# First attention of a gated cross-attention kernel: setup in 64-row bands, turned value-output rows, loads in halves, mask written by ScalarE

## The reference, cut to what matters

```
q = layernorm(x) @ wq[h] + bq[h];  k = ctx @ wk[h] + bk[h];  v = ctx @ wv[h] + bv[h]
scores = where(mask[b, s, t], q @ k.T / sqrt(64), -1e9)
out    = concat_h(softmax(scores) @ v) @ wo + bo
x      = x + tanh(g_xattn[0]) * out
```

## Time and profile before

| | |
|---|---|
| median of 3 runs | 776.97 us (775.05 to 778.43) |
| the profiled execution | 778.79 us, its span 777.0 us |
| TensorE busy | 735.8 us, 95% of the span |
| DVE, ACT, POOL busy | 415.7, 255.4, 120.4 us |
| mean granted TensorE clock | 0.983 |
| first weight-fed matmul | 5.93 us |
| first scores matmul of the first attention | 45.88 us |
| one tile in the steady loop | 10.80 us |

### The profile page before, as it was taken

The page is one execution under the profiler, slowest core; times in us unless marked ns, Lnnn a source line. Parts: engine busy times, 40 slices in busy tenths (PEclk is TensorE's granted clock), DMA queues, the critical chain, the costliest instruction groups (busy, mean ns, idle before and its releaser), DMA issues. The chain is left out here.

```text
span 777.0 us, 11690 instructions
## 1 busy us (share of the span) xinstructions
PE 735.8 (95%) x3507; PEld 500.0 (64%) x3508; DVE 415.7 (53%) x1020; ACT 255.4 (33%) x544; POOL 120.4 (16%) x129
## 2 busy tenths in 40 slices
PE   6989999999989999799999999999999999999991
PEld 6857776677754344589998756555665665665661
DVE  5868766776734475998889443212333333333330
ACT  1532323222245444657776331111211211221220
POOL 4100000000000000100000005540223223223222
PEclk9999999999999999999999899999999999999997
DMA  9534000000014000029001102322222322322221
GB/s 305 139 124 152 0 0 1 0 0 0 0 60 158 0 0 1 1 96 339 0 0 55 28 1 96 111 82 69 41 48 41 48 48 41 47 48 41 45 37 20
DMA packets 42401, 45.11 MB, mean 58 GB/s; under 512 B 8404, under 2 KB 36134, under 8 KB 42372
## 3 DMA queue, kind: packets, MB, share of 16 engines
q1 hardware_dynamic: 35028, 34.99, 14.4%
q0 software_dynamic: 7344, 9.75, 7.6%
HBM read 27.91 MB, written 16.79 MB: 58 GB/s over the span
## 5 line engine op out<-in xcount | busy, mean ns | idle before, releaser
L408 PE MATMUL ps<-middle,work 128*128 128x256 f32 (+3 forms) x824 | 217.7, 410 | 2.2 <-ACT work L960 1.5
L960 ACT ACTIVATE work<-ps 128x256 f32<-128x256 f32 (+5 forms) x263 | 100.9, 420 | 343.7 <-PE ps L411 315.9
L408 PEld LDWEIGHTS ps<-middle,work 128*128 128x128 f32 x824 | 152.1, 190 | 42.4 <-issue 23.6
L408 PE MATMUL ps<-early,work 128*128 x312 | 141.1, 595 | 0.8 <-ACT work L960 0.8
L411 PE MATMUL ps<-consts_sb,work 128*128 128x128 f32 (+1 forms) x672 | 99.1, 282 | 13.0 <-ACT work L960 3.9
L411 PEld LDWEIGHTS ps<-consts_sb,work 128*128 128x128 f32 (+1 forms) x672 | 78.6, 142 | 48.6 <-issue 28.3
L408 PEld LDWEIGHTS ps<-early,work 128*128 128x128 f32 x312 | 57.8, 190 | 61.7 <-issue 60.5
L408 PE MATMUL ps<-late,work 32*128 32x154 f32 (+3 forms) x704 | 81.8, 309 | 2.3 <-DVE x_rows L1471 1.1
L1702 DVE COPY work<-ps 128x256 f32<-128x256 f32 x39 | 16.6, 425 | 117.7 <-PE ps L411 117.7
L408 PE MATMUL ps<-early,late 128*128 128x512 f32 (+2 forms) x192 | 78.1, 611 | 0.3 <-ACT early L1061 0.3
L372 POOL TENSOR_TENSOR rstd<-var_eps,minus_half 128x8 f32<-128x8 f32 (+2 forms) x8 | 13.4, 1672 | 415.6 <-DVE var_eps L1270 415.6
(11 more groups left out here) (159 smaller groups left out, 608.8 us busy)
## 6 DMA issues: line engine op xcount, KB each, us to landing
early<-in_w SPq DMA_DIRECT2D x16, 512.0 KB, 10.3
expert_rows<-work SPq DMA_DIRECT2D x39, 130.0 KB, 2.7
work<-expert_rows SPq DMA_DIRECT2D x39, 130.0 KB, 2.1
middle<-in_w SPq DMA_DIRECT2D x8, 512.0 KB, 8.1
x_rows<-in_x SPq DMA_DIRECT2D x4, 512.0 KB, 9.4
out_rows<-x_rows SPq DMA_DIRECT2D x4, 512.0 KB, 3.1
late<-in_ws SPq DMA_DIRECT2D x3, 512.0 KB, 3.8
early<-in_wv SPq DMA_DIRECT2D x1, 1024.0 KB, 9.4
```

Source lines behind the costliest of these rows:

```text
L408: return nc.tensor.matmul(o, l, r, start=start, stop=stop, **kw)
L960: return nc.scalar.activation(o, i, ACT.Copy)
```

## The change

In the setup, `kbd` and `zv` go. K and V are written whole to `ks` and `vs` (one DVE addition a bank in place of four), and each head is multiplied alone: a `unit(n)` does its three or two pairs as two bands of 64 rows, one head each, both batches side by side (154 columns), the two bands into two banks. ACT evicts the even heads (`even_rows`), DVE the odd ones (`odd_rows`). Units 0 to 5 make `gk`; units 6 to 11 make the value side transposed, `voT`, and 40 transposes on TensorE (`turn_out`, ten groups of two chunks) turn it into `vo`, evicted seven groups by ACT and three by DVE. Units 8 to 11 and the turns come after the first tile's scores.

The row bq . k goes too, with its splitting and its DMAs. Instead each row of `wq_s` is shifted so that it sums to bq (`shift`, from row sums by ACT with an accumulator and by DVE), and ACT adds 1.0 to each transposed normed tile. Since a normed row sums to zero, the shift alone adds nothing, and the 1.0 adds bq . k.

The mask is converted by POOL, turned once by 16 bf16 matmuls of 77 columns into `seed0`, and ACT copies a tile's 77 columns (`pick`) and writes them, spread over the heads, into the scores' banks before the f32 matmuls add to them (`seeds0`). Only the first tile keeps the bf16 mask matmul. Loads of K, V and Q come in halves, x in four parts, and the statistics of x are made in three parts (two tiles a batch in the setup, the others after the first and the second tile's step). Four matmuls on zeros (`warm`) open TensorE's program.

```diff
 # SyncE
-            for a, z in ((0, 3 * P), (3 * P, H * DK)):
-                sp.dma_start(wk_s[:, :, a:z], wk0[:, a:z].rearrange("(k p) n -> p k n", p=P)).then_inc(q[f"ld_k{a // 384}"], 16)
-            sp.dma_start(wv_s, wv0.rearrange("(k p) n -> p k n", p=P)).then_inc(q["ld_v"], 16)
-            sp.dma_start(wq_s, wq0T.rearrange("(j p) n -> p j n", p=P)).then_inc(q["ld_q"], 16)
+            weights(wk_s, wk0, 0, "ld_k0")
+            weights(wk_s, wk0, 1, "ld_k1")
+            sp.dma_start(wq_s[:, 0:4, :], wq_rows[:, 0:4, :]).then_inc(q["ld_q"], 16)
+            weights(wv_s, wv0, 0, "ld_v0")
+            tiles(0, 2, "ld_x0")
+            weights(wv_s, wv0, 1, "ld_v1")
+            sp.dma_start(wq_s[:, 4:8, :], wq_rows[:, 4:8, :]).then_inc(q["ld_q2"], 16)
             sp.dma_start(wo_s, wo0.rearrange("(j p) n -> p j n", p=P)).then_inc(q["ld_o"], 16)
...
 # GpSimd
-            nc.gpsimd.memset(zv.rearrange("p b n -> p (b n)"), 0.0).then_inc(q["pool_fill"], 1)
-            nc.gpsimd.memset(mlhs[:], 1.0).then_inc(q["pool_fill"], 1)
+            nc.gpsimd.tensor_copy(id_bf, ident[0:NK, 0:NK]).then_inc(q["mask_done"], 1)
+            pool.wait_ge(q["ld_mask"], 32)
+            nc.gpsimd.tensor_scalar(mlhs[:], mask_u8[:], BIG, -BIG, ALU.mult, ALU.add).then_inc(q["mask_done"], 1)
+            pool.wait_ge(q["su_shift"], 2)
+            for j in (6, 7):
+                nc.gpsimd.tensor_tensor(wq_s[:, j, :], wq_s[:, j, :], shift[:, j:j + 1].to_broadcast([P, D]),
+                                        ALU.add).then_inc(q["su_w2"], 1)
...
 # TensorE
+            def unit(n):
+                after(pe, q["su_ea"], FREE_EVEN[n])
+                after(pe, q["su_ed"], FREE_ODD[n])
+                u, m = n % 6 // 2, n % 2
+                left, right = ((wq_s, ks), (wo_s, vs))[n // 6]
+                j0, j1 = 3 * u, min(3 * u + 3, PAIRS)
+                for j in range(j0, j1):
+                    for r in range(2):
+                        rows = slice(64 * r, 64 * r + 64)
+                        last = mm(ps[:, UNIT_BANKS[n][r], PW * (j - j0):PW * (j - j0) + PW],
+                                  left[rows, j, P * m:P * m + P], right[rows, j, :])
...
                 for u, (a, z) in enumerate(UNITS):
-                    after(pe, q["n_sub"], 3 * t - 2 + u)
                     n = NK * (z - a)
+                    if seeded:
+                        pe.wait_ge(q["n_seed"], 3 * t - 2 + u)
+                    else:
+                        mm(ps[:, u, 0:n], mlhs[:, p, 0:P], spread(id_bf, 1, [NK, z - a, NK]), True, True)
                     for m in range(KD):
-                        mm(ps[:, u, 0:n], xnT[p][:, m, :], gk[:, p, m, NK * a:NK * z], m == 0, False)
-                    mm(ps[:, u, 0:n], mlhs[:, p, bass.ds((i + k // 2) * P, P)], mrhs[p][:, NK * a:NK * z],
-                       False, True).then_inc(q["n_sc"], 1)
+                        last = mm(ps[:, u, 0:n], xnT[p][:, m, :], gk[:, p, m, NK * a:NK * z], False, m == KD - 1,
+                                  skip_group_check=True)
+                    last.then_inc(q["n_sc"], 1)
...
             xt0(0, 0)
-            step0(0, 0, prev=False)
+            scores0(0, 0, seeded=False)
+            xt0(0, 1)
+            for n in range(8, 12):
+                unit(n)
+            for g in range(len(TURNS)):
+                turn_out(g)
+            scores0(0, 1)
...
 # ScalarE, in each step of the loop
+            def seeds0(i, k, units):
+                t = 2 * i + k
+                if units[0] == 0:
+                    act.wait_ge(q["n_seeds"], 3)
+                    copy(pick[:, k % 2, :], seed0[:, bass.ds(tile_of(i, k), 1), :].rearrange("p a n -> p (a n)")
+                         ).then_inc(q["n_pick"], 1)
+                    act.wait_ge(q["n_pick"], t)
+                for u in units:
+                    a, z = UNITS[u]
+                    act.wait_ge(q["n_sub"], 3 * t - 2 + u)
+                    copy(ps[:, u, 0:NK * (z - a)].rearrange("p (h t) -> p h t", t=NK),
+                         spread(pick[:, k % 2, :], 1, [P, z - a, NK])).then_inc(q["n_seed"], 1)
...
                 if nxt:
                     ev_xt(i, k + 1)
+                    seeds0(i, k + 1, (0, 1))
                 exps(i, k, "n", DK ** -0.5)
+                if nxt:
+                    seeds0(i, k + 1, (2,))
```

More of the change, by code:

```diff
@@ L426, in _ @@
[L426 to L434 removed]
+            project(0, 0)
+            pe.wait_ge(q["ld_k1"], 16)
+            project(0, 1)
@@ new lines, in _ @@
+            act.wait_ge(q["ld_q"], 16)
+            for j in range(4):
+                last = nc.scalar.activation(cut(middle, D * j, [D]), wq_s[:, j, :], ACT.Copy, accum_out=wsum[:, j:j + 1])
+            last.then_inc(q["su_wsum"], 1)
+            act.wait_ge(q["su_shift"], 1)
+            shifted(0, 4)
+            for n in range(3):
+                act.wait_ge(q["n_seed_mm"], n + 1)
+                t0, t1 = 6 * n, min(6 * n + 6, T)
+                copy(seed0[:, t0:t1, :].rearrange("p t k -> p (t k)"),
+                     ps[:, (6, 7, 0)[n], 0:NK * (t1 - t0)]).then_inc(q["n_seeds"], 1)
@@ L986, in su1_turned @@
+            for n in range(8):
+                even_rows(n)
             def su1_turned(b):
@@ L1376, in step0 @@
                 soft(i, k, "n")
+                if not prev:
+                    for n in range(8, 12):
+                        odd_rows(n)
+                    dve.wait_ge(q["gate_done"], 1)
+                    for g in TURNS_DVE:
+                        turned_out(g)
                 dve.wait_ge(q["n_exp"], 2 * i + k + 1)
```

384 lines of the change are left out of this document (217 added, 167 removed).

## The result

The change took 759.0 us in the median of 4 runs (757.57 to 763.87) beside 777.7 for the kernel before on the same chip (4 runs, 775.05 to 779.76): 0.9749 of it, interval 0.9717 to 0.9782. Forecast: 760.5, with 755 to 767 as the range. The profiled execution took 757.79 us, its span 756.0.

What follows compares the result with a forecast made beforehand. TensorE was taken to bound the kernel; a lead of 12.1 us plus 5.4 in the loop gave 17.5, from the median 776.97 to 759.5, plus 1.0 for hand-overs: 760.5 us, range 755 to 767.

Steps and rivals of the forecast that it cites:

- Setup, TensorE's work: Setup: 30.4 us of TensorE work removed; banded units at 0.85 and 0.6 us and 40 transposes at 4.5 added.
- bands in file: Setup rival: 64-row bands don't overlap, units cost 1.6 and 1.0 us, first scores at 29.7, time 766.3; chance 0.08.
- POOL: Setup: mask conversion takes 2.7 us, between 1.82 and 4.09, mask ready at 13.8; two shift additions 0.65 each.
- Chain: Setup to seventh tile: first scores 25.9, second 40.8, a 1.5 us wait at the fourth tile, lead 12.1 us.
- Loop: First attention's steady loop: without mask matmuls a step takes 10.26 us, not 10.80; the rest of the loop saves 5.4.
- So they cost nothing: Steady loop: ACT's seeds, 1.8 us a step, are ready when due, and DVE's ring keeps 1.3 us of room.
- a late seed would hold TensorE one for one: Steady loop: if the seeds' time cover were gone, each delay of a seed would delay TensorE equally.
- The allowance: Chain: 1.0 us added to the forecast for some forty hand-overs between engines, of which few were counted.
- POOL holds TensorE: Setup rival: conversion 4.09 us, additions 1.3 each, clock costing up to 3; time 763.2 to 766; chance 0.13.
- The start binds less: Setup rival: less waiting or no 1.5 us stall, lead 15 not 12.1; time 757.5 or 756.5; chance 0.10.
- Seeds in the ring: First attention rival: seeds in series with DVE, ring 12.4 us a tile, time 785; chance 0.05, slower than before 0.03.
- Turns eat it: Setup rival: turns with 40 transposes and ten more evictions eat the bands' saving, lead 5 us, time 767; chance 0.06.

Runs made afterwards that it cites:

- 5: The changed kernel run once more without any edit: 763.7 us, ratio 0.9801 to the kernel before.
- 9: The changed kernel with every matmul of the twelve units issued twice in a row: 769.8 us, ratio 0.9881 to the kernel before.
- 10: The changed kernel with no warm matmuls, and with seven in place of four, one run each: 764.1 and 765.1 us.
- 4: The changed kernel with mask row and some statistics moved into DVE's waits, POOL's first inverse deviation ahead of its additions: 762.2 us, ratio 0.9785.
- 1: The changed kernel with the bf16 mask matmul back in every tile and no ACT seeds in the first attention: 764.6 us, ratio 0.9836.
- 6: On top of 4, ACT's exponential put ahead of the next tile's seeds from the fifth tile on: 758.6 us, ratio 0.9738.
- 7: The changed kernel with each ACT seed preceded by an unread copy of the same size to SBUF: 769.1 us in one run.
- 8: The changed kernel plus end strips of 154-column matmuls: ten records per 1 us window on one band, ten on 128 rows, twenty alternating; time not compared.
- 3: The changed kernel with loads in the old order, still in halves (K, V, Q, output weights, x last): 770.6 us, ratio 0.9893.
- 11: The kernel of 6 plus five unread f32 matmuls of 256 columns in TensorE's last wait of the first attention: 757.6 us, ratio 0.9737.

## Why the prediction was right, point by point

The forecast was right in its sum, and nearly in every step. What it had wrong were sizes of opposite sign. The sum took 16.5 us off the median of before; the traces show 16.0 to the end of the loop, and the medians lie 18.7 and, in 5, 16.9 apart. How near a median of few runs comes to 760.5 is in part luck, since runs of one kernel differ by six microseconds.

- **Setup, TensorE's work.** Four figures don't follow from their rows. The removed work is 2 x 2.26 + 8.67 + 14.94 = 28.1 us, not 30.4; a low end of 0.77 for a unit is below 3 x 0.27 = 0.81; the value side's six units come to 4.6 at the prices taken, not 4.1; and in the rival of bands in file units 8 to 11 are 2.3 longer, not 2.0. The forecast uses none of them; that rival's 766.3 would have been 766.6. Units took 0.81 and 0.54 where 0.85 and 0.6 were taken (9). The 16 small mask matmuls were priced too high: 0.72 us, not 1.4. The 40 turns are 3.28 + 1.53 us long, 4.5 were taken. Six matmuls of a unit in less than 1 us, as announced: 1.84 for two units. Drains at the change between full and banded use, up to 1.2 us together in the prediction, are smaller here. At 17.30, 24.37 and 30.33 the first record of the new use starts 0.06 to 0.07 us before the last of the old one ends, where most other neighbours overlap by 0.16: about a tenth of a microsecond at each, if the modelled ends can be trusted so far.
- **POOL.** The conversion, taken at 2.7 between 1.82 and 4.09, took 1.89: the low end. (Mask at 10.8 and 2.7 make 13.5, not the 13.8 of the prediction.) Its two additions took 0.6 each (0.65). The conversion, then, is nearer to the memset of the same size than I put it, and that it also reads cost 0.07 us. The Trainium skill's figure for an addition of 2048 f32 with two inputs on this engine (GPSIMD Engine Reference, Performance versus the Vector engine) did not carry over to one input: the 1.89 us decides. It brought nothing, because V's first half was late: forecast to land at 10.6, it landed just before 11.88 by the wait in 10, and K, forecast to end at 10.2, ended at about 12.1 (14.51 less the 2.37 of half a V). So the mask matmuls began at 14.34, not 13.8. The short mask matmuls took that back, and V's second half ended at 17.3 (17.2).

```profile
10.29 1.89 POOL L393 TENSOR_SCALAR masks<-masks 77x2048 bf16<-77x2048 uint8 x1 [0.99 <-DMA mask_row_u<-in_mask]
```

- **Chain.** First scores 25.33 (25.9), second 40.09 (40.8), the fourth tile's wait 1.48 (1.5), its transposes at 66.65 (67.0 for the product), a step 10.24 (10.26), the seventh tile's scores at 93.3 (93.7): a lead of 12.4 where 12.1 stood. The claim that this one wait is left over from DVE's late start holds: without it (4) the transposes come 1.37 earlier.
- **Loop.** Ten steps gave 5.4 us to TensorE as the sum has it (17.8 at the last transposes, 12.4 before). **The step that failed is "So they cost nothing":** it looked only at when the seeds are due on TensorE, not at the exponential, ahead of which two of them were put. In the steady loop that is hidden, for DVE's product (the row below) ends at 115.86, still 2.1 us before the transposes that read it, at 117.94. At the last tile nothing hides it, because DVE's chain from the sum to the last `soft` is the path there: 1.3 us, and 0.5 more that TensorE saves beside that chain. 17.8 became 16.0; experiments 1, 6 and 7 show it (1.8 less loss than TensorE's saving; 1.3 gained back; 1.0 more lost). The rule "a late seed would hold TensorE one for one" came to bear only in 7, once, with 0.29 us; in the change the first two seeds end 2.3 us before the scores that need them (111.48, and 117.94 - 4.13 = 113.81).

```profile
114.42 1.44 DVE L1513 TENSOR_TENSOR work<-work,rden 128x1232 f32<-128x1232 f32 x1
```

- **The allowance.** 1.0 us for hand-overs was more than setup and steady loop needed (they came out 0.3 better than the sum), and stands by luck near the 1.8 given back: the sum with it was 16.5, the traces say 16.0.
- **Rivals.** Bands in file: excluded by 8 and 9. POOL holds TensorE: excluded by the rows above. Its part on the clock did not come in the change's setup (1.00 throughout), but it was right in kind: it came in the setups of 3 and 7, for 3.5 and 1.6 us, and at the seams. The start binds less: no, 1.48 is there. Seeds in the ring: excluded, 7 even with twice the writing. Turns eat it: no; they cost about 1.0 us more than without seeds between them (1).
- **A price not asked for.** The order of the loads was put down as in the sum; undone, it cost 7.2 us in the trace of 3. Half of that is waiting, because the order decides what stands first in DVE's queue, and half is the clock that fell in that wait.

## What to carry to other kernels

A piece of work put on an idle engine is priced by what stands behind it in that engine's queue, and at the last step of a loop, where no slack is left, not only by when its own result is due: put it behind the operation that the chain waits for, if its due time allows. Contractions of 64 rows pay only if work for the other half of the array stands close by: one and one or two and two ran at the double rate, three and three did not, one half alone gained nothing. All these runs gave each half a bank of its own; one bank for both was not tried. Load order is an order of queues too: see whose engine a late transfer blocks, and for whom, and count what a wait of TensorE may cost behind it in clock.

## What the runs showed of the hardware that was not expected

- At the seam behind the last tile, with waits of TensorE of 1.2 and 2.5 us just before, the granted clock was 1.00 in the change, 0.87 and 0.79 in its repeat, 0.66 in 4, 0.89 and 0.77 in 6 (stretches of 5 us). Of the thirteen executions that had the longer of these waits, it was 1.00 in six. That is up to 1.7 us for eight matmuls (5.30 to 3.60), and the repeat had 0.50 and 0.55 at 300 to 310 on top. Most of the spread of three microseconds each way between runs may come from such seams; this was seen in single traces, not counted. With the last wait filled it was 1.00 in the one trace of 11, which nearly one in two were without.
- Behind a wait of 3.88 us in the setup (3) the granted clock was 0.50 for ten microseconds, although TensorE was busy for most of them, and 64-row matmuls then came at about half their rate.
- At the start, four matmuls ran at half pace (3.78 us for four of 256 columns, where such a matmul later takes 0.44), TensorE then waited 1.28 us, and K's first matmuls were again slow, six records in the window 7 to 8 us, as in the kernel before. The column of granted clock reads 1.00 from 7 to 8 us all the same. With seven and no wait K took 4.39 us. But with four, K also took 4.44 us in four executions, behind waits of 1.22 to 1.66 us, and was slow in seven, behind waits of 0.65 to 1.48. So the length of the wait does not decide it, and what does stays open.
- Writing 462 columns from ACT into PSUM took 0.54 us and 308 took 0.41, to SBUF 0.57 to 0.59 and 0.44 (7): the target made little difference.
